# A fused windowed attention and router on one core: keys ahead of values, another order of the work on every engine, output in pieces

## The reference, cut to what matters

```python
q = Wq @ layernorm(x);  k = Wk @ ctx;  v = Wv @ ctx         # 256 x 256 weights, 8 heads of 32 channels
dots = einsum('bhdt,bhdtw->bhtw', q, windows(k)) * scale    # 16 positions around each t, zero padded
out  = Wo @ einsum('bhtw,bhdtw->bhdt', softmax(dots), windows(v))
x1 = x + tanh(g_xattn) * out
h  = layernorm(x1)                                          # over the 2048 positions
scores = softmax(h @ router_weight.T + router_bias)         # 64 experts, one row of 2048 per channel
w  = the 8 largest of scores, the others 0
result = x1 + tanh(g_ffn) * (h * sum(w) + w @ expert_bias)
```

## Time and profile before

| | |
|---|---|
| median of 3 runs | 1551.26 us |
| the profiled execution, its own time | 1557.26 us |
| its span, first to last instruction | 1555.1 us |
| PE busy | 1464.6 us, 94% of the span |
| DVE, ACT, POOL busy | 1276.5, 1144.8, 1148.0 us (82%, 74%, 74%) |
| granted TensorE clock, mean | 0.972 of 2.4 GHz |
| DMA queue of SP | 206.14 MB, 49.1% of 16 DMA engines |

### The profile page before, as it was taken

How to read it: one execution, slowest core, us unless ns; L and a number is a source line. 1 busy time by engine, 2 the same in 40 slices (tenths; PEclk the granted TensorE clock), 3 DMA queues, 4 the chain that set the end, 5 groups by cost and what they waited for, 6 DMA issues and landing times.

```text
span 1555.1 us, 66658 instructions
## 1 busy us (share of the span) xinstructions
PE 1464.6 (94%) x28162; PEld 1199.9 (77%) x28162; DVE 1276.5 (82%) x2970; ACT 1144.8 (74%) x2009; POOL 1148.0 (74%) x1110
## 2 busy tenths in 40 slices
PE   4799999999999999999999999999999999999985
PEld 3687887888787888878788788878888887778764
DVE  5578987888898887988888898888889888788764
ACT  4687877777787877788787877778787787767652
POOL 4688777787777877877787887778778777677661
PEclk8899999999999999999999999999999999899896
DMA  7455455445546554454555545455554545434132
GB/s 230 125 140 126 106 173 131 123 149 143 147 121 172 141 131 146 121 157 128 149 149 141 156 119 159 128 146 147 144 159 114 159 132 142 121 98 128 44 81 85
DMA packets 365577, 210.39 MB, mean 135 GB/s; under 512 B 294497, under 2 KB 295521, under 8 KB 361057
## 3 DMA queue, kind: packets, MB, share of 16 engines
q1 hardware_dynamic: 365280, 206.14, 49.1%
HBM read 136.88 MB, written 33.55 MB: 110 GB/s over the span
## 4 chain that ended last, share of the span: by engine, by line
PE 46%; DVE 35%; issue 8%; POOL 5%; ACT 3%; DMA 2%; SPq 1%; POOLq 0%; DVEq 0%; ACTq 0%
PE ps_j L1117 18%; PE ps_s L1177 7%; PE ps_a L1142 6%; PE ps_r L1219 5%; DVE prob_t L900 5%; PE ps_s L1117 3%; DVE p_sum L890 3%; DVE st_x L907 2%; DVE wq_lo L822 2%; POOL prob L493 2%; DVE lg L1046 2%; DVE st_in L804 2%; DVE v_turn L871 2%; PE ps_s L1172 2%; PE ps_a L1196 2%
## 5 line engine op out<-in xcount | busy, mean ns | idle before, releaser
L486 POOL TENSOR_TENSOR score<-score,p_inv 128x384 f32<-128x384 f32 x256 | 221.6, 866 | 119.5 <-DVE p_inv L894 117.0
L493 POOL TENSOR_TENSOR prob<-score,prob 128x384 f16<-128x384 f32 x256 | 266.0, 1039 | 38.8 <-ACT prob L644 38.3
L1177 PEld LDWEIGHTS ps_s<-kv_win,q_col 32*32 32x32 f32 x16384 | 198.0, 107 | 57.8 <-issue 57.8
L1177 PE MATMUL ps_s<-kv_win,q_col 32*32 32x48 f32 x16384 | 234.1, 205 | 2.4 <-issue 2.2
L900 DVE STREAM_TRANSPOSE prob_t<-prob 128x512 f32<-128x512 f32 x256 | 176.7, 699 | 55.1 <-POOL prob L493 54.9
L467 POOL TENSOR_TENSOR c_lo<-c_in,c_hi 128x1024 fp32r<-128x1024 f32 x64 | 152.7, 2386 | 89.5 <-ACT c_hi L618 89.5
L1142 PEld LDWEIGHTS ps_a<-prob_t,v_diag 128*128 128x128 f16 x6528 | 175.3, 98 | 50.1 <-DVE prob_t L900 32.6
L1142 PE MATMUL ps_a<-prob_t,v_diag 128*128 128x48 f16 (+2 forms) x6528 | 187.6, 183 | 26.2 <-DVE prob_t L900 19.4
L462 POOL TENSOR_TENSOR att_lo<-att,att_hi 128x512 fp32r<-128x512 f32 x128 | 161.8, 1275 | 51.5 <-ACT att_hi L604 50.3
L1117 PE MATMUL ps_j<-c_hi,wkv_hi 128*128 128x512 f32 x512 | 171.3, 416 | 19.6 <-DVE kv_win L864 10.6
L890 DVE TENSOR_REDUCE p_sum<-score 128x8 f32<-128x384 f32 x256 | 139.2, 544 | 54.3 <-ACT score L638 53.6
(11 more groups left out here) (149 smaller groups left out, 3318.0 us busy)
## 6 DMA issues: line engine op xcount, KB each, us to landing
v_diag<-v_turn SPq DMA_DIRECT2D x512, 68.0 KB, 2.8
c_in<-ctx_dram SPq DMA_DIRECT2D x64, 512.0 KB, 4.9
x_in<-x_dram SPq DMA_DIRECT2D x64, 512.0 KB, 5.5
x_res<-x_dram SPq DMA_DIRECT2D x64, 512.0 KB, 4.3
out_dram<-x SPq DMA_DIRECT2D x32, 1024.0 KB, 7.0
c_sq<-ctx_dram SPq DMA_DIRECT2D x60, 512.0 KB, 5.5
x<-ctx_dram SPq DMA_DIRECT2D x4, 512.0 KB, 6.1
x<-experts_dram SPq DMA_DIRECT2D x2, 512.0 KB, 10.6
```

Of the source, the lines that this page charges most:

```text
L486: pool.tensor_tensor(score[:, u], score[:, u], p_inv[:, u, :].unsqueeze(2).to_broadcast([P, HALF, KEYS]), ALU.mult).then_inc(pm_rdy, 1)
L493: pool.tensor_tensor(part(prob[:, u % 2], 1)[:, :, 0:KEYS], score[:, u], part(prob[:, u % 2], 0)[:, :, 0:KEYS], ALU.subtract).then_inc(pl_ ...
L1177: ins = pe.matmul(s[head(h), n * KEYS:(n + 1) * KEYS], q_col[head(h), g, at:at + SUB], kv_win[c % 2][head(h), 0, g, at:at + KEYS], start=F ...
```

## The change

It does the following.

1. **PE's list.** In a step `scores(0)` and `rows(1)` now stand ahead of `attend(0)`; `scores(1)` ahead of `router`; `keys` where `values` stood, and `values` last. `keys` no longer waits for the evictions of the values, and `values` waits for `kh_rdy`, the eviction of the keys. The four `mixture` calls are spread one by one. A chunk's values are evicted, and their low part made, in the next step. Sixteen matmuls over `wr` become a `tensor_reduce` on DVE and one matmul.
2. **Halos apart.** POOL's `halo` is called for the values (middle of the step) and for the keys (end of the step), each with semaphores of its own.
3. **DVE, ACT, POOL.** Other orders. `turn(0)` comes ahead of `total(2)`, `values_turn` moves from the head of the step to behind `invert(1)`, `next_stats(0)` stands ahead of `turn(2)`. `normalise(3)`, `low(2)`, `low(3)` and `high(2)`, `high(3)` go to the head of the next step. The low part of the query weights goes from DVE to POOL, made of a copy that ACT writes. `router_weights` is no longer interleaved. The experts' parts go from POOL to ACT and DVE, in the first sequence.
4. **Router's tiles in PSUM.** `wd` is the logits' place in `ps_r` itself, `lg` another part of that bank. So the next router may only write when `wd_rdy` says the weights are done.
5. **SP's list.** `c_in`, `c_sq`, `v_diag` of g = 0, `x_in`, `v_diag` of g = 1, `x_res`, and an output row block as four DMAs of a chunk each. `c_sq` is loaded one step earlier. Ahead of step -2, `c_in` and x[0] move forward.

The diff, cut to its core:

```diff
+        wd = ps_r[:, LOGITS:LOGITS + G * E].rearrange("p (g e) -> p g e", g=G)
+        lg = ps_r[:, G * E:2 * G * E].rearrange("p (g e) -> p g e", g=G)
...
+                def diagonal(g):
+                    need(sp, vt_rdy[g], nth(b, c, 0))
+                    need(sp, av_mm[g], nth(b, c, -1))
+                    for h in range(HPG):
+                        sp.dma_start(v_diag[head(h), g, :, head(h)],
+                                     v_turn[head(h), g].rearrange("p (j d) -> p j d", d=SUB)).then_inc(vd_ld[g], 16)
...
+                if live(b, c, 0):
+                    diagonal(0)
+                if live(b, c, 5) and live(b, c, 1):
+                    ch, db = place(c, 5)
+                    rows_in = x[b + db, :, cols(ch)].rearrange("(g p) t -> p g t", g=G)
+                    need(sp, xl_rdy, nth(b, c, 1))
+                    sp.dma_start(x_in[:, :, cols(ch)], rows_in).then_inc(x_ld[ch], 16)
+                if live(b, c, 0):
+                    diagonal(1)
...
-                    rows_out = out[b - 1, g * P:(g + 1) * P, :]
-                    need(sp, fin_rdy, final(b - 1, g, NCH - 1))
-                    sp.dma_start(rows_out, x1[1 - par][:, g, :]).then_inc(out_st[g], 16)
+                    for j in range(NCH):
+                        rows_out = out[b - 1, g * P:(g + 1) * P, cols(j)]
+                        need(sp, fin_rdy, final(b - 1, g, j))
+                        sp.dma_start(rows_out, x1[1 - par][:, g, cols(j)]).then_inc(out_st[g], 16)
...
+                def queries_weight_low():
+                    need(pool, wqh_rdy, b + 2)
+                    pool.tensor_tensor(wq_lo[:], wq_ln, wq_hi[:], ALU.subtract).then_inc(wql_rdy, 1)
...
-            def queries_weight_low(b):
-                need(dve, wqh_rdy, (b + 1) * G)
-                for g in range(G):
-                    dve.scalar_tensor_tensor(wq_lo[:, g], wq_raw[:, g], rs_in[:, g:g + 1], wq_hi[:, g],
-                                             ALU.mult, ALU.subtract).then_inc(wql_rdy, 1)
...
-                        dve.scalar_tensor_tensor(lg[:, g, 0], wd[:, g, 0:E], rs_x1[:, g:g + 1], rb[:],
-                                                 ALU.mult, ALU.add).then_inc(small, 1)
+                            dve.scalar_tensor_tensor(lg[:, g], wd[:, g], rs_x1[:, g:g + 1], rb[:],
+                                                     ALU.mult, ALU.add).then_inc(small, 1)
...
+                def keys(g, off):
+                    need(pe, cl_rdy, nth(b, c, off))
+                    if live(b, c, off - 3):
+                        need(pe, ob_rdy[g], nth(b, c, off - 3))
+                    else:
+                        need(pe, vl_rdy[g], nth(b, c, off - 1))
+                    project(ps_j[g], wkv_hi[:, 0], wkv_lo[:, 0], g, c_hi, c_lo).then_inc(k_mm[g], 1)
+                def values(g, off):
+                    need(pe, kh_rdy[g], nth(b, c, off))
...
-                    need(pe, vl_rdy[g], nth(b, c, 2))
-                    project(ps_j[g], wkv_hi[:, 0], wkv_lo[:, 0], g, c_hi, c_lo).then_inc(k_mm[g], 1)
```

More of the change, by code:

```diff
@@ L523, in step @@
-                if now:
-                    low(3)
+                    halo(0, 1, kr_rdy, kl_rdy, kh_rdy)
+                if b == -1 and c == 2:
+                    constants()
             walk(step)
@@ L627, in centre, with x_high @@
                                        bias=neg_mean_in[:, g:g + 1]).then_inc(xc_rdy, 1)
-                def x_high():
-                    ch, _ = place(c, 1)
-                    need(act, xc_rdy, done(2, b, c, 1, 1))
+                def x_high(off):
+                    ch, _ = place(c, off)
+                    need(act, xc_rdy, nth(b, c, off) * G)
+                    for g in range(G):
+                        need(act, q_mm[g], nth(b, c, off - 1))
+                    act.activation(x_hi[:], x_in[:, :, cols(ch)], ACT.Copy).then_inc(xh_rdy, 1)
@@ L748, in _ @@
+                if b == 0 and 1 <= c < 3:
+                    half = slice((c - 1) * (T // 2), c * (T // 2))
+                    act.activation(ex_hi[:, half], ex_staged[:, half], ACT.Copy).then_inc(exh_rdy, 1)
             walk(step)
@@ new lines, in step @@
+                if live(b, c, 0) and c == 1 and seq(b + 1):
+                    scales(b + 1, 1 - par, 2)
+                if live(b, c, 0):
+                    largest(1, 0)
+                if live(b, c, 0) and c == 1 and seq(b + 1):
+                    scales(b + 1, 1 - par, 3)
+                if live(b, c, 1):
+                    values_low(1, 1)
+                if live(b, c, 0) and c == 1 and seq(b + 1):
+                    scales(b + 1, 1 - par, 4)
+                if live(b, c, 0):
+                    total(0, 0)
+                    invert(0, 0)
+                    shift(1, 0)
+                    largest(2, 0)
+                    shift(2, 0)
@@ L951, in step @@
                 if finishing(b, c):
                     finish(0)
-                if now:
-                    largest(2)
-                    shift(2)
+                if c == 1 and seq(b - 1):
+                    router_logits(b, 0)
+                if live(b, c, 0):
+                    total(1, 0)
+                if c == 1 and seq(b - 1):
+                    router_logits(b, 1)
+                if live(b, c, 0):
+                    invert(1, 0)
+                if c == 1 and seq(b - 1):
+                    router_logits(b, 2)
@@ L976, in step @@
-                if scaling:
-                    scales(b + 1, 1 - par, 1)
+                if live(b, c, 0):
+                    shift(3, 0)
+                    turn(0, 0)
+                    total(2, 0)
+                    invert(2, 0)
+                if live(b, c, -1):
+                    stats_x1(0, -1)
+                if live(b, c, 0):
+                    total(3, 0)
+                if live(b, c, -1):
+                    stats_x1(1, -1)
+                if live(b, c, 0):
+                    invert(3, 0)
@@ L994, in step @@
-                if live(b, c, 2):
-                    values_low(0)
-                    values_low(1)
-                if routing:
-                    router_weights(b, 0)
+                if live(b, c, 0):
+                    turn(1, 0)
                 if finishing(b, c):
                     finish(3)
-                if now:
-                    total(3)
-                if routing:
+                if c == 1 and seq(b - 1):
+                    router_weights(b, 0)
+                if c == 0 and seq(b - 1):
+                    ln2(b)
@@ L1309, in _ @@
+                if b == 0 and c == 0:
+                    pe.wait_ge(wrp_rdy, 1)
+                    pe.matmul(ps_r[:, WRSUM], all_ones[:], wr_part[:], start=True, stop=True).then_inc(sum_mm, 1)
             walk(step)
```

1119 lines of the change are left out of this document (542 added, 577 removed).

## The result

The changed kernel takes 1579.31 us (median of 4 runs, 1574.33 to 1586.43), the kernel before 1551.85: ratio 1.0164, 95% interval 1.0140 to 1.0188. It is 27 us slower where 25 us less were forecast. The loss is under 2%, but its interval is clear of 1. The profiled execution took 1574.33 us, its span is 1572.5.

A forecast was written before the change was run, and what follows sets the result against it. PE's own work was taken as the bound. Gains of 7 (start), 12 (middle), 5 (late part) and 1.5 us (last store), 25.5 in all, took 1557.3 to 1531.8; the median lies 6.0 lower: 1526 us, range 1507 to 1555.

The forecast's parts named there:

- SP's list: Middle: turn(3) waits behind x_in, issued after four v_diag DMAs; margin 1.8 us, 0.3 in c = 1.
- DVE, ln2 and the router's weights: Middle: the subtraction moved to POOL can stop small DVE instructions, 2.20 us a stop; left in the range.
- The middle's gain: From 88 to 1348 us: PE's waits go, 1.0 us idle and 0.2 switching per sequence for 2.1: 12 us gained.
- The start: Step 0: c_sq loaded earlier, scores(1) at about 52.4 for 56.69, less time at lower clock: 7 us gained.
- Late part and last store: From 1348 to 1511 us, turn waits shortened: 5 us gained; last store in pieces at the end: 1.5 us.
- Tiles in PSUM: DVE's chain in c = 1: 275 in place of 946 ns, 1.3 us per sequence, only shortening waits already counted.
- my fourth rival: Tiles in PSUM do not help; PE waits 1 us once per sequence in the middle: 1540 us, chance 0.1.
- The slower rival: Middle: attend(1) waits behind turn(3) behind a late x_in and the clock falls: 1578 us, chance 0.12.
- the three cases and the half rival: Faster than 1548 us: forecast 0.45, all idle time gone 0.2, PSUM 0.1, half of idle time stays (0.13); given as 0.78.

The follow-up runs named there:

- k1: The changed kernel with SP also waiting for the end of scores(2) ahead of the loads of c_in and c_sq: 1549.36 us, ratio 0.9967.
- k4: The kernel before with SP issuing c_in and c_sq at the head of a step, ahead of the eight v_diag DMAs: 1579.04 us, ratio 1.0147.
- k2: e1 with SP's loads of c_in and c_sq behind the end of scores(2): 1518.99 us, ratio 0.9775.
- k3: k2 with the router's weights spread over step c = 1 and next_stats(0) behind the turns on DVE: 1504.32 us, ratio 0.9680.
- e1: The changed kernel with ln2's root in PSUM, so its Newton steps read at most one operand from SBUF: 1556.04 us, ratio 1.0013.
- m2: k3 with the output of a half stored as one 1 MB DMA, not four of 256 KB: 1506.09 us, ratio 0.9700.
- e3: The changed kernel with the eight stages of router_weights spread over step c = 1 in place of one piece at its end: ratio 1.0023.
- e4: The changed kernel with next_stats(0) behind turn(2), turn(3) and largest(0) on DVE: ratio 0.9993.
- h4: e1 with only c_sq issued behind the first four v_diag DMAs, c_in still at the head of the step: 1604.24 us, ratio 1.0355.

## Why the prediction was wrong, step by step

- **SP's list: this is the step that failed.** The prediction followed `x_in` behind `v_diag` and asked whether it lands in time. It left out that `c_in` and `c_sq` now go ahead of `v_diag`, at the head of the step, and what else uses the DMA engines then. Its cost was taken as nothing; k1 and k4 measure 28 and 25 us, in stalls of PE and in the lower clock that follows some of them. The DMA share of 0.53, on which I leaned, is a mean: in the stretch that counts it is full.
- **DVE, ln2 and the router's weights: this failed too.** The sum put it at nothing. The prediction had the price of a stop (2.20 us) and the rule for it, but looked only at the subtraction that came to POOL, not at where POOL's old instructions went: `normalise(3)`, `low(2)`, `low(3)` and behind them `context_low` stand at the head of the next step, beside ln2. With the loads in place this costs 30 us (k1 against k2), and the router's weights and `next_stats(0)` 15 more (k2 against k3). The prediction left it in the range, but with the loads held back the kernel is at 0.9967 (k1), some 20 us above the forecast. So either of the two steps alone would have spoilt it. The rule of the Trainium skill (SBUF — State Buffer, "Who interferes with whom"), that a DVE instruction with two SBUF inputs waits for a GpSimd one that reads SBUF, holds here: 2.35 us beside a 2.40 us subtraction, and 0.28 us for e1's form, with the root in PSUM.
- **The middle's gain.** The waits for the values' low part did go (of the 18 in the earlier trace rows one of 0.5 us is left), and the idle time of about 14 us that I forecast is there, and less (8.1), in k3, which has both losses taken out and two more changes of order. So the mechanisms of that term hold as far as this shows; the two that were not in it were larger. With them 40.4 us were lost, 12 of them to the clock, against 12 gained in the forecast.
- **The start.** Right: `scores(1)` of step 0 begins at 50.36 us (the first row below, of PE) in place of 56.69 and of the 52.4 forecast, 6.3 us gained there and 9.4 by the fifth step, for 7. ACT no longer waits for `c_sq` there. `scores(0)` of this step was to stay near 49 us and begins at 46.85, which I had not seen.
- **Late part and last store.** Right in sign; the late part was put too small: from 1326.37 and 1357.30 to the last matmul (1549.3 and 1568.4) it is 223 and 211 us, 12 gained for 5. SP's last wait is 1.6 us (the second row) for 3.4, near the 1.5 forecast; m2 is too coarse to tell it.
- **Tiles in PSUM.** 282 ns, as read from L1041. I gave the time nothing for them; they are worth about 12 us once DVE's chain is what PE waits for. That is the size of my fourth rival (14 us).
- **The slower rival** gave 1578 us, and its place is right, `attend(1)` behind `turn(3)`. Its cause is wrong: not `x_in`, but POOL. It also had the clock fall, from waits of about 2 us on, and take 2.3 us in each sequence; the clock did fall, but behind one wait of 1.62 us and five stalls of 1.3 to 2.6 us, and took 12 us more than before in 13 sequences. And it had nothing of the loads. That the number fits is luck.
- **The chances.** Those of the three cases and the half rival that I call faster add up to 0.81 or 0.82, not to 0.78.

```profile
50.36 0.34 PE L1176 MATMUL ps_s<-mask,ident_b 128*128 128x384 bf16 x1 [0.78 <-ACT q_col L586]
```

```profile
SPq L418 <- DMA out_dram<-x: 1.6, 1, 1.6
```

- **Left open.** How much of e3's and e4's surplus is the clock; when the clock falls behind a wait and when not; and what lets the loads' 512 KB in h4 do as much harm as 1 MB.

## What to carry to other kernels

Ask of each load that is moved not only whether it lands in time, but what PE does while it runs: in a stretch of many small matmuls PE also needs its own program from the same DMA engines, and one wait that holds 1 MB back for 8 us was worth 28 us. Read the granted clock beside the idle time: short stalls cost more than they last when it falls behind them. List what POOL runs beside each chain of small SBUF instructions on DVE; each can last as long as POOL's instruction. After a wait is removed, look again, since the next one was beneath it.
